# Four selective-scan blocks on one core: B's diagonal matrices read from a DRAM image, and the chunk loop written out

## The reference

```
x_dbl = x_proj_weight[k] @ u                      # rank + 16 (B) + 16 (C) rows per position
dt    = softplus(dt_projs_weight[k] @ x_dbl[:rank] + bias[k])
h     = exp(dt * A[k]) * h + dt * B * u           # per channel (384) and state (16), along L
y     = sum over the states of h * C, + D * u     # summed over the 4 directions
```

## Time and profile before

| | |
|---|---|
| median of 3 runs | 31304.53 us (31281.53 to 31306.0) |
| profiled execution | 31304.37 us, span 31302.4 us |
| busy: PE, DVE, POOL, ACT | 93%, 87%, 76%, 61% |
| mean granted TensorE clock | 0.963 |
| scans of DVE (L831) | 18432, 1258 ns or 1199 ns |
| products for `diag` (L812) | 1536, 1199 ns |

### The profile page before, as it was taken

One profiled execution on the slowest core, in us unless ns is written; L12 is line 12 of the kernel. 1 busy time (PEld: TensorE's weight loads), 2 busy tenths in 40 slices (PEclk: granted clock), 3 DMA queues, 4 the chain that ended last, 5 costly groups with the idle time before them and its releaser, 6 DMA issues. The chain is left out here.

```text
span 31302.4 us, 684367 instructions
## 1 busy us (share of the span) xinstructions
PE 29091.5 (93%) x247872; PEld 20808.3 (66%) x247872; DVE 27266.5 (87%) x25017; ACT 19120.8 (61%) x38088; POOL 23928.4 (76%) x10772
## 2 busy tenths in 40 slices
PE   9999998998999999899899989989989999998998
PEld 6775775774677577577467757757746775775774
DVE  8987997996898799799689879979968987997996
ACT  5665664664666566466466656656646665664664
POOL 7885985894788598589478869858847885985884
PEclk9999999998999999999899999999989999999998
DMA  1111111121111111112111111112111111111121
GB/s 64 68 61 48 67 66 51 70 72 33 65 67 61 48 67 67 51 70 71 34 66 66 61 49 66 68 50 71 70 34 66 66 61 48 66 68 50 70 71 33
DMA packets 373333, 1881.34 MB, mean 60 GB/s; under 512 B 111332, under 2 KB 115644, under 8 KB 165928
## 3 DMA queue, kind: packets, MB, share of 16 engines
q1 hardware_dynamic: 345448, 1792.34, 16.2%
q10 hardware_dynamic: 24384, 42.48, 0.4%
HBM read 1740.26 MB, written 94.37 MB: 59 GB/s over the span
## 5 line engine op out<-in xcount | busy, mean ns | idle before, releaser
L877 POOL TENSOR_TENSOR regB<-regB,regA 128x1024 f32<-128x1024 f32 x9216 | 21630.3, 2368 | 2844.0 <-ACT carry L707 2815.6
L831 DVE TENSOR_TENSOR_SCAN regB<-regB,carry,ps 128x512 f32<-128x512 f32 x16128 | 19237.2, 1258 | 889.7 <-PE ps L584 345.9
L584 PEld LDWEIGHTS ps<-regA,regB 64*128 64x128 f32 x147456 | 9069.7, 189 | 4928.2 <-DVE regB L831 2723.7
L718 ACT ACTIVATE regB<-regB,a_neg 128x512 f32<-128x512 f32 x18432 | 12192.5, 710 | 30.0 <-issue 30.0
L584 PE MATMUL ps<-regA,regB 64*128 64x128 f32 x147456 | 10844.0, 287 | 797.7 <-DVE regB L831 654.4
L598 PE MATMUL ps<-ident,regB 128*128 128x128 f32 x73728 | 10172.1, 281 | 45.5 <-POOL regB L877 29.5
L598 PEld LDWEIGHTS ps<-ident,regB 128*128 128x128 f32 x73728 | 7978.8, 142 | 1177.7 <-issue 43.9
L707 ACT ACTIVATE carry<-regB 128x2 f32<-128x2 f32 x9216 | 1886.3, 205 | 7922.4 <-DVE regB L831 7869.3
L867 POOL TENSOR_TENSOR regB<-regB,u 128x512 f32<-128x512 f32 x1152 | 1622.1, 1408 | 2065.0 <-DVE regB L801 2065.0
L831 DVE TENSOR_TENSOR_SCAN regB<-regB,ps 128x512 f32<-128x512 f32 x2304 | 2621.4, 1199 | 173.4 <-PE ps L584 171.9
L812 DVE TENSOR_TENSOR regA<-fold,ps 128x1024 f32<-128x1024 f32 x1536 | 1808.7, 1199 | 366.8 <-PE ps L558 366.8
(11 more groups left out here) (83 smaller groups left out, 15885.7 us busy)
## 6 DMA issues: line engine op xcount, KB each, us to landing
regA<-xd SPq DMA_DIRECT2D x1536, 1024.0 KB, 4.8
regA<-x_in SPq DMA_DIRECT2D x16, 1536.0 KB, 14.6
x_keep<-regA SPq DMA_DIRECT2D x8, 3072.0 KB, 18.8
regA<-x_keep SPq DMA_DIRECT2D x16, 1536.0 KB, 16.2
regB<-xd SPq DMA_DIRECT2D x128, 192.0 KB
xd<-regB ACTq DMA_DIRECT2D x96, 256.0 KB
xd<-regB ACTq DMA_DIRECT2D x192, 88.0 KB
regB<-w_in_in SPq DMA_DIRECT2D x28, 576.0 KB, 4.9
```

Source lines behind the costliest of these rows:

```text
L584: mm = nc.tensor.matmul(ps[:, 2 * (g % 2) + i, q * 2 * RT:(q + 1) * 2 * RT], dtuT[at, up, q, :], diag[at, cp, q, g], start=True, stop=True)
L718: nc.scalar.activation(decays[:, g % 2, s], dt[:, up, :], ACT.Exp, scale=a_neg[:, c[0], d, 2 * g + s:2 * g + s + 1]).then_inc(a_made, 1)
L831: nc.vector.tensor_tensor_scan(ring[:, g % RING, s, way], decays[:, g % 2, s, way], b[:, s, way], 0.0 if begun else carry[:, d, at:at + 1] ...
L877: nc.gpsimd.tensor_tensor(ring[:, g % RING], ring[:, g % RING], c_all[:, g], ALU.mult).then_inc(g_made, 1)
```

## The change

DRAM gets, per block, `b_dram` (B of each chunk, once more) and `eye_dram`, two images of 128 x 4096 fp32, each written with zeros once at the start of the kernel. Whoever stores a chunk's projection also stores B's rows to `b_dram` in the order quarter, state, position (`store_b`). ACT then issues, for the next chunk, two DMAs from `b_dram` to the image's diagonals (`spread`, at d = 0, g = 4): each has 64 x 64 single elements, with a step of 4097 elements down the diagonal. SP waits for these and loads the image into `diag` with one DMA of 128 x 16 KB (`load_diag`), between the loads of dt's rows and of C. `load_b`, `turn_b` and `make_diag`, with `brow` and `fold`, are gone. The image has the 64 columns of each state together, so `inputs` hands the matmul an output view with a step of two elements. The hardware loops over chunks, in the stage ahead of them on ACT too, are written out.

```
+            zeros = regA[:, 0:QS * NS * RT]
 
             @block.sync
             def _(sp):
                 sp.dma_start(ident[:], ident_in).then_inc(loaded, 16)
-                sp.dma_start(fold[:], fold_in).then_inc(loaded, 16)
                 sp.dma_start(group_mean[:], group_in).then_inc(loaded, 16)
                 sp.dma_start(chan_mean[:], ones_in).then_inc(loaded, 16)
-                sp.wait_ge(loaded, 64)
+                sp.wait_ge(loaded, 48)
+                sp.wait_ge(zero_set, 1)
+                for c in range(2):
+                    sp.dma_start(eye_dram[c, 0:P * EYE].rearrange("(p x) -> p x", p=P), zeros).then_inc(zeroed, 16)
+                sp.wait_ge(zeroed, 32)
...
-                    step(chunk_of(k, 0, 0), before, chunk_of(k, 1, 0), 0)
-                    with eng.Fori(0, NCH // 2 - 1) as j:
-                        c = [chunk_of(k, j * 2 + i, j + i // 2) for i in range(4)]
-                        step(c[1], c[0], c[2], 1)
-                        step(c[2], c[1], c[3], 0)
-                    step(chunk_of(k, NCH - 1, NCH // 2 - 1), chunk_of(k, NCH - 2, NCH // 2 - 1), after, 1)
+                    c = [chunk_of(k, n, n // 2) for n in range(NCH)]
+                    for n in range(NCH):
+                        step(c[n], c[n - 1] if n else before, c[n + 1] if n + 1 < NCH else after, n % 2)
...
+            def store_b(eng, k, n, rows, sem):
+
+                eng.dma_start(b_dram[l][k, n].rearrange("(a n r) -> n a r", n=NS, r=RT),
+                              rows.rearrange("n (a r) -> n a r", r=RT)).then_inc(sem, 16)
...
+                    def load_diag(c, cp):
+                        S = c[3]
+                        sp.wait_ge(spread_b, (S + 1) * ROWS * 16)
+
+                        wait(sp, b_made, (S - 1) * NDB * PAIRS)
+                        sp.dma_start(diag[:, cp].rearrange("p q g t -> p (q g t)"),
+                                     eye_dram[cp, 0:P * EYE].rearrange("(p x) -> p x", p=P)).then_inc(diag_loaded, 16)
...
                             load_dts(after)
+                            load_diag(after, 1 - par)
...
-                                mm = nc.tensor.matmul(ps[:, 2 * (g % 2) + i, q * 2 * RT:(q + 1) * 2 * RT],
+                                b = ps[:, 2 * (g % 2) + i, q * 2 * RT:(q + 1) * 2 * RT]
+                                mm = nc.tensor.matmul(b.rearrange("p (t s) -> p s t", s=2),
                                                       dtuT[at, up, q, :], diag[at, cp, q, g],
                                                       start=True, stop=True)
...
+                    def spread(c, cp):
+
+                        k, n, _, S = c
+
+                        wait(act, spread_b, S * ROWS * 16)
+                        if k == 0:
+                            act.wait_ge(xd_pre, (PRE_FREE + n + 1) * 32)
+                        else:
+                            act.wait_ge(xd_stored, (S - NCH + 1) * 32)
+                        rows = b_dram[l][k, n].rearrange("(i a r) -> i a r", i=ROWS, r=RT)
+                        for i in range(ROWS):
+                            onto = eye_dram[cp, i * RT * EYE:i * RT * EYE + RT * (EYE + 1)].rearrange(
+                                "(r x) -> r x", x=EYE + 1)[:, 0:EYE].rearrange("r (a b) -> a r b", b=RT)
+                            act.dma_start(onto[:, :, 0:1], rows[i].rearrange("a (r o) -> a r o", o=1),
+                                          allow_slow_non_contiguous=True).then_inc(spread_b, 16)
...
+                        if n == 2:
+                            spread(chunk_of(0, 0, 0), 0)
...
+                                    store_b(act, k + 1, n, xd_out[R:R + NS], xd_stored)
+                                if d == 0 and after and g == ACT_B:
+                                    spread(after, 1 - par)
```

More of the change, by code:

```diff
@@ L39 @@
 QS = T // (ROWS * RT)
-PE_LAG, PE_BT, PE_Z, PE_SKIP, PE_Y, PE_XD, PE_TR = 3, 0, 1, 4, 5, 5, 6
-ACT_XD, ACT_IN, ACT_LOG, ACT_YT, ACT_Y, ACT_TR = 0, 2, 3, 3, 6, 7
-DVE_DT, DVE_DIAG = 3, (1, 2, 4, 4)
+EYE = QS * NS * RT
+PE_LAG, PE_Z, PE_SKIP, PE_Y, PE_XD, PE_TR = 3, 1, 4, 5, 5, 6
+ACT_B, ACT_XD, ACT_IN, ACT_LOG, ACT_YT, ACT_Y, ACT_TR = 4, 0, 2, 3, 3, 6, 7
+DVE_DT = 3
 POOL_DTU = 3
@@ L69, in wait, with build @@
         eng.wait_ge(sem, value)
-def build(nc, x_in, ident_in, fold_in, group_in, ones_in, w_in, w_out, w_xp, w_dt, vecs, out):
+def build(nc, x_in, ident_in, group_in, ones_in, w_in, w_out, w_xp, w_dt, vecs, out):
     ctx = ExitStack()
@@ L144, in build @@
         xd_dram = [nc.dram_tensor(f"xd_{l}", (K, NCH, 1 + RANK[l] + 2 * NS, T), F32).ap() for l in range(3)]
+        b_dram = [nc.dram_tensor(f"b_{l}", (K, NCH, NS * T), F32).ap() for l in range(3)]
+        eye_dram = nc.dram_tensor("eye", (2, P * EYE + RT), F32).ap()
         x_dram = nc.dram_tensor("x_keep", (CB, NCB, L), F32).ap()
@@ L516, in step @@
                         if after:
-                            sp.wait_ge(bt_mm, after[3])
                             if after[0]:
-                                sp.wait_ge(xd_stored, (after[3] - NCH + 1) * 16)
-                            load_b(after)
+                                sp.wait_ge(xd_stored, (after[3] - NCH + 1) * 32)
                             load_dts(after)
+                            load_diag(after, 1 - par)
                             for h in range(PAIRS // 2):
@@ L551, in project_dt @@
                                          dts[0:R + 1], start=True, stop=True).then_inc(z_mm, 1)
[L553 to L561, removed]
                     def turn_dtu(c, d):
@@ L647, in step @@
                                     sums(*old, par_of(old[0], par, this, old[1]))
-                                if d == 1 and g == PE_BT and after:
-                                    pe.wait_ge(dtT_made, unit(this, 1) + 1)
-                                    turn_b(after)
                                 if nxt and g == PE_Z:
@@ L666, in step @@
                                 if nxt and g == PE_TR:
-                                    if d == 1 and after:
-                                        pe.wait_ge(diag_made, (S + 2) * QS)
                                     pe.wait_ge(dtT_made, unit(this, d) + 1)
@@ L742, in _ @@
                                              scale=dsum[:, d:d + 1])
-                    with act.Fori(0, NCH // 2) as j:
-                        for q in range(2):
-                            n = j * 2 + q
-                            act.wait_ge(xd_mm, n + 1)
-                            act.wait_ge(xd_pre, (n + 1) * 16)
-                            nc.scalar.activation(xd_sb2[0:M, q, :], ps[0:M, 3 + 4 * q, :],
-                                                 ACT.Copy).then_inc(xd_copied, 1)
+                    for n in range(NCH):
+                        act.wait_ge(xd_mm, n + 1)
+                        act.wait_ge(xd_pre, (n + 1) * 32)
+                        nc.scalar.activation(xd_sb2[0:M, n % 2, :], ps[0:M, 3 + 4 * (n % 2), :],
+                                             ACT.Copy).then_inc(xd_copied, 1)
+                        if n == 2:
+                            spread(chunk_of(0, 0, 0), 0)
                     first = chunk_of(0, 0, 0)
@@ L771, in step @@
                                     act.wait_ge(xd_mm, S + NCH + 1)
-                                    wait(act, xd_stored, S * 16)
+                                    wait(act, xd_stored, S * 32)
                                     nc.scalar.activation(xd_out[0:M], ps[0:M, Z_BANK, :],
@@ L837, in _ @@
                     first = chunk_of(0, 0, 0)
-                    for q in range(QS):
-                        make_diag(first, q, 0)
                     make_dt(first, 0, 0)
@@ L848, in step @@
                                     make_dt(*nxt, par_of(nxt[0], par, this, nxt[1]))
-                                if d == 1 and after:
-                                    for q in range(QS):
-                                        if g == DVE_DIAG[q]:
-                                            make_diag(after, q, 1 - par)
                     chunks(dve, step)
```

47 lines of the change are left out of this document (14 added, 33 removed).

## The result

The changed kernel takes 30,199.7 us (median of 4 runs, 30,197.8 to 30,209.6), the kernel before 31,300.0 (31,281.5 to 31,306.0): a ratio of 0.9652, interval 0.9638 to 0.9666, so 1,100 us or 3.5% less. The forecast was 36,000 us, range 30,300 to 37,900. Both the sign and the range were wrong.

What follows compares the result with a forecast made beforehand. PE and DVE were taken to bound a chunk together, within 1 us, DVE alone in direction 3. 31304 - 632 (loop) + 5232 (stepped write) + 85 (once and per scan) = 35,989, say 36,000 us; range 30,300 to 37,900.

Steps and rivals of the forecast that it cites:

- Part 1, the loop: Hardware loop over chunks: written out, all 384 chunks run straight, saving 52.7 us a scan over 12 scans, -632 us.
- Part 2, the products and turn_b: make_diag leaves DVE, turn_b leaves PE: 1.0 us a chunk saved, some 3 us in direction 3, 576 us in all.
- Part 3, the stepped write: L584 writing PSUM at a step of two doubles its streaming time: +15.6 us of PE a chunk, +5232 us net.
- the rival with the hold all covered: Stepped write in PSUM free and ACT's hold fully hidden: 30,180 us; the faster rival as a whole had 28%.
- the dear side: Case that L584's stepped PSUM write slows like a stepped read, giving the forecast time of 36,000 us; chance 45%.
- Part 4, the hold: ACT's second spread issue held 3.2 to 15.7 us a chunk; taken as 0 if L584's longer blocks cover it.
- The rival by hold alone: Stepped write free, but ACT's spread costs about 50 ns a piece: 32,870 us, 31,400 to 35,200; chance 22%.
- Part 5, the image load: 2 MB a chunk on SP's queue, about 10 us, lands before the next chunk: 0 us added.
- Part 6, once and per scan: Two 2 MB stores at the start, +25 us, and each scan's first image load, +60 in all: together +85 us.

Runs made afterwards that it cites:

- loop written out: Kernel before with only the loop over chunks written out on every engine, products for diag and contiguous write kept: 30,684.2 us, ratio 0.981.
- changed, no spread in the chunks: Changed kernel issuing only the first spread of each scan, image load kept, B wrong in the output: 29,985.4 us, ratio 0.9583.
- changed, four buffers: Changed kernel with four buffers and four semaphores, not two and one, for projections stored ahead of a scan's first chunk: 30,133.4 us, ratio 0.9632.
- four buffers, spread split: Four-buffer version of the changed kernel with the spread's second DMA issued four half steps later, at d = 1, g = 0: 29,912.7 us, ratio 0.9559.

## Why the prediction was wrong, step by step

The traces, one execution of each kernel, can be divided into the time inside the scans (in each of the 12 executions of `scan`, from the start of DVE's first scan instruction to that of its last) and the rest, in us:

| kernel | inside the scans | outside | span |
|---|---|---|---|
| before | 25,899 | 5,404 | 31,302 |
| loop written out | 25,291 | 5,391 | 30,682 |
| changed | 24,734 | 5,474 | 30,208 |
| changed, no spread in the chunks | 24,522 | 5,468 | 29,989 |
| changed, four buffers | 24,732 | 5,400 | 30,132 |
| four buffers, spread split | 24,519 | 5,400 | 29,918 |

*Part 1, the loop: right.* -632 forecast, -594 measured alone by the medians, -608 inside the scans. Reading "issue" waits at a loop's back-jump, and comparing looped with straight chunks of the same trace, sized it within 7%.

*Part 2, the products and turn_b: too small by a quarter.* -576 forecast (1.0 us a chunk, 3 us in direction 3). From the written-out kernel to the changed one the time inside the scans falls by 557 us, which looks right but is so by luck: that figure has ACT's hold in it. Without the spread it falls by 769, 2.0 us a chunk instead of 1.5, and the hold takes 212 back. By the starts of the scans, a chunk that is neither the first nor the last of its direction fell (written out, then without the spread) from 66.4 to 65.1 us in directions 0 and 2, from 66.1 to 64.4 in direction 1, and from 66.1 to 61.5 in direction 3. In direction 3 this is because DVE's 4.3 us and PE's 1.6 us both came out and PE became the bound. That directions 0 to 2 gave more than the 1.0 us was not forecast, and why is not shown.

*Part 3, the stepped write: the step that failed.* It added 15.6 us to a chunk and replaced part 2, +5,232 us instead of -576, and it carries the error: 35,989 less that difference of 5,808 is 30,181, the rival with the hold all covered. The reasoning was that "a stepped write doubles L584 the same way" as the read of the earlier trace rows. Three runs say no: the block of 16 is at 1.09 us with the step, taking the step out brings 13 us, and the isolated matmul takes 10.52 us with it and without it. Two things were missed in it. The row was unlike the edit in kind and in size: it reads at a step of 64, while the edit writes at a step of 2, and at step 2 even the read costs 5%. And the row's contiguous rate, 0.84 ns a column, was read as "no slack"; it is slow enough to hide the step, as the same write in bf16, which streams at 0.43 ns a column, does double. The Trainium skill (PSUM — Partial Sum Buffer, Specifications (TRN2)) says that any non-contiguous pattern slows matmuls; these runs bear that out for bf16 writes (2.78 to 5.34 us) and not for fp32 writes at steps 2, 4 and 8, so the measurement decides. The trace of before could not settle it, but 45% on the dear side was more than one unlike row and one general sentence justified.

*Part 4, the hold: its size right at the low end, its cover and its way wrong.* Forecast 3.2 us and more for the second issue by 17 ns a piece, 0.35 for an issue by itself; measured 3.58 by the timeline (2.9 in the median) and 0.53. By the prediction's sum for 17 ns 0.6 us a chunk would show, 230 us; 214 did. The forecast itself put this at 0, as it counted on part 3's longer blocks to cover it. And the trace shows DVE waiting for the decays in 14 half steps only; what it does show is the carry copy, POOL and then PE's sums (125.2 against 29.5 us), 96 of the 214. The way of the rest is open. The rival by hold alone is out: it needs 31 ns or more a piece.

*Part 5, the image load: right.* 7.7 us to land (10 forecast), and without it the chunks are equally long.

*Part 6, once and per scan: right in size.* +85 forecast. Outside the scans the changed kernel takes 83 us more than the written-out one and 70 more than the kernel before. Four buffers for the projections' stores bring 74 of them back, and leave the time inside the scans as it was.

So the rival at 30,180 came within 20 us of 30,200 by two errors of some 200 us each that cancelled: the products were worth 769 us and not 576, and 212 us of hold showed where it had none. That part of the agreement is luck; the free write and the price of the loop are not.

## What to carry to other kernels

When the price of an operation is taken from a row that is like it but not the same, check in what it differs (read or write, size of the step, data type) before putting most of the chance on it; in these runs a stepped PSUM write cost nothing where the columns came at 0.84 ns anyway (fp32) and doubled the time where they came at 0.43 (bf16). When a sum comes out right, check its terms one by one, as two wrong ones can cancel. A DMA of thousands of tiny pieces may cost the chunk nothing in bandwidth and yet hold the engine that issues the next one: put the issues so far apart that the first has landed. And a hardware loop on the engine that bounds is worth timing as straight code.

## What the runs showed of the hardware that was not expected

- TensorE writes of PSUM with a step: free in fp32 at steps 2, 4 and 8 (10.52, 5.52 and 20.77 us, as contiguous), twice the time in bf16 (2.78 to 5.34 us for 24 of 256 columns).
- TensorE reads of SBUF with a step: +4 to 5% at step 2 in bf16 and fp32 (5.60 against 5.38 us, 21.81 against 20.77), double at steps 4 and 16 in fp32 (43.36 and 41.35 us).
- VectorE writing SBUF with neighbouring fp32 elements 64 apart: 1984 instead of 1199 ns for 1024 elements a partition.
- A DRAM to DRAM DMA of 4096 pieces of 4 bytes: 21 to 25 ns a piece on each of 16 engines where several queued; the next issue on the same engine takes 2.9 us in the median behind one such DMA (3.58 in the timeline shown) and 6.4 behind two or three (5.4 shown), instead of 0.53.
